# Asking for an expert's weights on the landed count of the row transfers

## The reference, cut to what matters

```
xd = jnp.zeros((E, CAP + 1, D), x.dtype).at[e_flat, slot].set(x[tok])
h = _relu2(jnp.einsum('ecd,eid->eci', xd, w1))
yd = jnp.einsum('eci,edi->ecd', h, w2)
y_assign = yd[e_flat, slot] * gate
return jnp.zeros((T, D), x.dtype).at[tok].add(y_assign)
```

## Time and profile before

| what | value |
|---|---|
| median of 3 runs | 998.89 us (996.33 to 1003.96) |
| the profiled execution | 995.25 us |
| its span, from first to last instruction | 993.4 us |
| TensorE busy | 892.7 us (90%) |
| GpSimd busy | 450.9 us (45%) |
| mean granted TensorE clock | 0.963 |
| mean DMA rate over the span | 144 GB/s |
| the expert stage's scatters, first and last start | 585.7 and 987.0 us |

### The profile page before, as it was taken

How to read it: one execution, slowest core, us unless ns; L and a number is a source line. 1 busy time by engine, 2 the same in 40 slices (tenths; PEclk the granted TensorE clock), 3 DMA queues, 4 the chain that set the end, 5 groups by cost and what they waited for, 6 DMA issues and landing times. The chain is left out here.

```text
span 993.4 us, 14519 instructions
## 1 busy us (share of the span) xinstructions
PE 892.7 (90%) x4913; PEld 627.3 (63%) x4913; DVE 564.3 (57%) x1148; ACT 232.5 (23%) x716; POOL 450.9 (45%) x499
## 2 busy tenths in 40 slices
PE   4799999988899999869998999999899899998990
PEld 3566666664677777766443376868586668575850
DVE  4788878867688888876999722223233223222220
ACT  1455656461400000123110011111111111111110
POOL 1644452533588888620160134444445445344432
PEclk9989999999999999979999999999999999998995
DMA  7300000020533333033070158988998899789963
GB/s 290 112 1 2 1 2 1 2 75 1 210 105 100 96 92 92 0 128 128 0 275 0 60 177 259 270 254 222 290 277 259 220 271 290 214 225 298 275 149 53
DMA packets 44125, 143.40 MB, mean 144 GB/s; under 512 B 7280, under 2 KB 11632, under 8 KB 35120
## 3 DMA queue, kind: packets, MB, share of 16 engines
q1 hardware_dynamic: 26352, 96.46, 26.4%
q0 software_dynamic: 14912, 37.76, 19.4%
q10 hardware_dynamic: 2816, 8.59, 2.3%
HBM read 114.36 MB, written 28.43 MB: 144 GB/s over the span
## 5 line engine op out<-in xcount | busy, mean ns | idle before, releaser
L1346 PE MATMUL ps<-arena 128*128 128x128 f32 (+4 forms) x2128 | 521.1, 403 | 13.6 <-DVE arena L791 5.7
L1346 PEld LDWEIGHTS ps<-arena 128*128 128x128 f32 x2128 | 340.9, 192 | 156.7 <-issue 111.9
L574 POOL DMA_INDIRECT out<-arena,scatter_rows x64 | 101.8, 1590 | 208.6 <-DMA out<-arena,scatter_rows 144.3
L1281 DVE TENSOR_TENSOR arena<-arena 128x256 f32<-128x256 f32 x64 | 27.3, 427 | 221.3 <-ACT arena L776 208.3
L1346 PE MATMUL ps<-features_T,arena 128*128 (+2 forms) x640 | 116.0, 338 | 0.0
L624 ACT ACTIVATE arena<-ps 128x512 f32<-128x512 f32 (+1 forms) x137 | 78.3, 590 | 134.9 <-issue 63.0
L1346 PEld LDWEIGHTS ps<-features_T,arena 128*128 128x128 f32 x640 | 84.7, 188 | 37.3 <-issue 37.3
L563 POOL DMA_INDIRECT arena<-token_rows,gather_rows x64 | 66.9, 1046 | 64.1 <-DVE gather_rows L1274 52.9
L465 POOL TENSOR_TENSOR arena<-arena 128x512 f32<-128x512 f32 x48 | 49.2, 1057 | 87.6 <-DVE arena L811 87.6
L776 ACT ACTIVATE arena<-ps 128x256 f32<-128x256 f32 x64 | 24.6, 384 | 247.1 <-PE ps L1346 231.1
L634 ACT ACTIVATE arena<-arena 128x128 f32<-128x128 f32 x192 | 74.0, 389 | 16.6 <-DVE arena L799 16.3
(11 more groups left out here) (173 smaller groups left out, 1069.5 us busy)
## 6 DMA issues: line engine op xcount, KB each, us to landing
arena<-wexp SPq DMA_DIRECT2D x48, 1024.0 KB
residual<-wexp SPq DMA_DIRECT2D x16, 1024.0 KB
arena<-toeplitz_rows SPq DMA_DIRECT2D x32, 256.0 KB, 3.1
arena<-ctxE SPq DMA_DIRECT2D x32, 192.0 KB, 3.2
residual<-x SPq DMA_DIRECT2D x4, 1024.0 KB, 5.3
token_rows<-arena SPq DMA_DIRECT2D x16, 256.0 KB, 2.0
arena<-suT ACTq DMA_DIRECT2D x1, 2048.0 KB, 7.9
arena<-sdT ACTq DMA_DIRECT2D x1, 2048.0 KB, 12.6
```

The lines of the kernel that those rows point to most:

```text
L574: pool.indirect_dma_start(out, bass.IndirectOffsetOnAxis(ap=idxs[:, s % NY:s % NY + 1], axis=0), ysb[:, s % NY, :], None, compute_op=ALU.a ...
L1346: ins = TE.matmul(out_ap, lhsT, rhs, start=(n == 0), stop=(n == len(pairs) - 1))
```

## The change

SyncE no longer waits for written descriptors, but for landed transfers. The weights of expert n are asked for when scatter n - 7 has landed, and the tile scatter too where it stands between n - 7 and n - 6 (`links_before` counts these links). The first such load, of expert 6, waits for the end of the first expert's output product. The loop over the experts is written out for 16 of them, where it was for 8, since the count of links differs within a group. GpSimd's one-column product, its wait and its semaphore go.

```
-                if s >= AHEAD:
-                    sp.wait_ge(scatter_begun, s - AHEAD + 1)
+                if s == AHEAD:
+                    sp.wait_ge(y_filled[0], 2)
+                elif s > AHEAD:
+                    sp.wait_ge(added, 16 * (s - AHEAD))
                 load_expert(s, 0)
-            with sp.Fori(1, E // UE) as i:
-                for s in range(UE):
-
-                    sp.wait_ge(scatter_begun, i * UE + (s - AHEAD + 1))
-                    load_expert(s, i)
+
+            def links_before(r):
+                return r + (1 if r == GROUP - 1 else 0)
+
+            for r in range(UE, GROUP):
+                sp.wait_ge(added, 16 * links_before(r - AHEAD))
+                load_expert(r % UE, 1)
+            with sp.Fori(0, E // GROUP - 1) as j:
+                for r in range(GROUP):
+
+                    late = r - AHEAD
+                    links = LINKS + links_before(late) if late >= 0 else links_before(GROUP + late)
+                    sp.wait_ge(added, j * (16 * LINKS) + 16 * links)
+                    load_expert(r % UE, j * 2 + (2 + r // UE))
...
-
-                if before is not None:
-                    pool.wait_ge(scatter_begun, i * UE + s)
-                G.tensor_tensor(begun_mark[:], minus_half[:, 0:1], minus_half[:, 0:1], ALU.mult).then_inc(scatter_begun, 1)
```

More of the change, by code:

```diff
@@ L99, in program @@
         tile_rows = sb("tile_rows", [P, NT // 4])
-        begun_mark = sb("begun_mark", [P, 1])
         AREA = 34400
@@ L270, in program @@
         scatter_landed = sem("scatter_landed")
-        scatter_begun = sem("scatter_descriptors_written")
         out_written = sem("result_rows_begun")
```

## The result

The changed kernel takes 1042.95 us in the median of 4 runs (1040.6 to 1046.85) against 1000.78 for the kernel before: ratio 1.0429, 95% interval 1.0373 to 1.0484. Its profiled execution took 1040.6 us with a span of 1038.8, 45.4 more than the span before.

What follows compares the result with a forecast made beforehand. The chain of scatter landings was taken to set the end; 56 ordinary links at +1.05 us each give +59 us, all else 0, on 995.25 us: 1054, given as 1055 us, forecast 1037 to 1075, range 1018 to 1118.

Steps and rivals of the forecast that it cites:

- SyncE ahead of GpSimd: Start of a link: SyncE's weight request would stand 0.7 us ahead of the scatter's start, not 2 us behind.
- the 1 us of the sum: After a landing: weights reach the DMA engines at 1.7 us, scatter's rows at 2.8, about 1 us later.
- The order at the DMA engines: DMA queues: a transfer coming second waits for nearly the whole load, so the scatter's rows wait out the weights.
- The price of a link: Ordinary expert link: 6.7 to 7.2 us, taken as 7.0, which is 1.05 over the mean before.
- The number of links: Expert stage: 56 ordinary links pay; tile links, the first loads and the last six count 0.
- The product: GpSimd's one-column product goes: gather starts up to 0.93 us earlier, worth 0 on the path that sets the end.
- The median landing, the DMA share: Profile after: scatter landing 6.2 us in the median instead of 4.8; DMA share falls to about 0.76.
- Rival (a): DMA engines were the bound and loads fill their gap: links 5.28 us, -38 us, 958 us; chance 0.07.
- Rival (b): Links cost what the seen slow ones cost, 8.15 us: +123 us, 1118 us; chance 0.2.
- Its clock argument: TensorE, with gaps in each link, often gets the lower clock: at half speed 11 us per expert, not 5.5.
- (c): Scatter slips in early on most DMA engines: link 6.3 us, +20 us, 1015 us; chance 0.08.
- (d): Change does nothing: request late for another reason, or rows go first; within 1%; chance 0.05.

Runs made afterwards that it cites:

- one pause: Changed kernel, with SyncE loading one 4-byte number and waiting for it ahead of each weight load; ratio 1.121, ordinary links 7.94 us in the median.

## Why the prediction was right

The direction and the step that carries it were right: both wait for the same landing, SyncE's way to the first byte is the shorter one, and the rows wait out the load.

- **SyncE ahead of GpSimd**: 0.7 us were forecast, 0.60 measured. The 1.6 us from issue to data were read off a load whose way was taken by the first scatter's rows. In the link shown the load's first 8 pieces start 1.0 us after the issue (716.2) and the ninth at 716.9, 1.6 us after it. So the first pieces are further ahead of the rows than the 1 us of the sum; the order comes out the same.
- **The order at the DMA engines**: as forecast from the gather behind its load. Of the two readings of the Trainium skill's rule ("DMA: Bandwidth & Descriptors", Queues, rings and completion order) the one with a packet as large as the engine's share is what the trace of one pause looks like: 103 pieces of the load start, and not one packet of the scatter, in the 2.7 us after the rows are due.
- **The price of a link**: mis-sized. I took 7.0 us from bounds of 6.7 to 7.2; the median is 6.61 and the mean 6.77, so 0.81 and not 1.05 over the mean before. The end of the load was right: in the link shown its last pieces start from 719.30 to 719.80, 4.3 to 4.8 us after the landing (715.85 - 0.8), where the sum had 4.7. Too large was what I added behind it, 2.3 us for the rows and 0.2 for the landing, less at most 0.5: the scatter lands 5.7 us after its start, 6.5 after the landing before, so 1.8 us behind those 4.7. The rows begin on some engines while others still load, and the slowest engine's load doesn't add to the whole of the rows. The mis-sized term is "the upper half, as the engines don't all finish their share together": the lower end was nearer, and the uneven finish shortens the sum instead of lengthening it, as I read it. By how much the waiting itself shortens the rows was not tried.
- **The number of links**: 56, and nothing for tile links, start and end, as counted. 56 x 0.81 = 45.5 against a forecast 59; the two times, 1043 and 1055, differ by nearly that.
- **The product**: 0 on the path, as forecast. But the gather did not start 0.93 us earlier: it starts 1.88 us after the scatter (717.73 - 715.85) where it was 1.94. The product had run mostly beside the descriptors' writing, not behind it; in the kernel before, in the link at 786.00, it starts 0.55 us ahead of the end of the scatter's instruction (787.56):

```profile
787.01 0.77 POOL L579 TENSOR_TENSOR begun_mark<-minus_half 128x1 f32<-128x1 f32 x1
```

  So GpSimd's idle time before a scatter is 3.6 us here and not 5: 0.9 of the difference because the gather starts no earlier, 0.5 because the link is shorter.
- **The median landing, the DMA share**: 5.8 us and 0.80, for a forecast of 6.2 and 0.76; both fit the shorter link (0.89 x 5.95 / 6.77 = 0.78).
- **Rival (a)**, a gap filled: refuted. Without any load a link is 5.57 us in the median and 5.61 in the mean, so there was no more to gain than 0.34 us of the mean, and the change gives the loads a worse place.
- **Rival (b)**, links of 8 us: not in the changed kernel, but it is what 0.6 to 1.1 us of further delay makes (7.44, 7.89, 7.94). Its clock argument has nothing in the runs for it, since in the slowest of them (clock 0.91 from 690 to 945) the chain waits for the load as the queues show.
- **Rivals (c) and (d)**: (c) gave 6.3 us for a link; the measured mean of 6.77 lies between it and the forecast, nearer the forecast. (d) didn't occur.

The slow links before (five of 7.5 to 10.2 us; after, there are six of 7.5 to 8.4) go with load pieces beside the rows, as the prediction read it from one of them: in each of the five, 13 to 31 pieces of a load start from 2.0 to 4.0 us into the link, in the 51 others 0 to 10 and once 15. What makes those pieces come then was not tried.

## What to carry to other kernels

Here a chain of small transfers sets the time and large loads share its DMA engines, and the place of the load's request within a link mattered more than how early it was. In such a kernel, ask while the chain's own packets are moving, so that they are ahead and the load is through before the next ones come. An instruction that looks idle may hold that place; before it is taken out, look at what its end triggers. A signal that comes earlier can make a load late for the chain in front of it, and one more half microsecond of delay can make it worse before it gets better.

## What the runs showed of the hardware

- A load whose first pieces start on the DMA engines holds back another queue's rows until it is nearly through: nothing of them in 2.7 us (one pause), and in 198 loads of four kernels no row ahead of the load's first 4-byte packet. The price of 1 MB in front of 128 rows of 2 KB is, in the median link over that of the kernel before, 1.0 us when it is asked for 0.6 us ahead of GpSimd's transfer, 1.8 when level with it, and 2.3 at 0.5 us behind.
- The first 8 pieces of a 1 MB load start 1.0 us after SyncE's issue, the others from 1.6 us (changed kernel, 716.2 and 716.9, asked for at 715.25).
- A bare semaphore increment behind an indirect transfer in GpSimd's queue lets SyncE issue with the start of that transfer's instruction (-0.03 us); one behind the next indirect transfer does so 0.5 us into the first, 1.4 us before the second starts. It says nothing of descriptors being written. A one-column product does: its end stands at 1.8 us, behind the 1.6 of the descriptors.
- A 4-byte load took 1.3 us from its issue to the next issue (733.83 to 735.17), and two in a row took 6.8 us behind a 1 MB load.
- The same one-column product shows 0.77 us beside the writing of descriptors, and 0.21 us where it stands behind the gather.
